# A convolution stage kept with features on partitions: centring folded into weights, variance by a matrix product

## Chip, cores and metric

One core of one Trainium2 chip runs the whole program. The metric is the device time of one execution in microseconds (us); less is better. The engines are TensorE (PE, its weight loads PEld), VectorE (DVE), ScalarE (ACT), GpSimd (POOL) and SyncE (SP, which issues the transfers).

## What is computed

The program is a chain of eight stages on 1024 tokens of 512 features, each followed by a residual sum and a layer norm. The change is in one of them, the convolution stack:

```python
h = einsum('blv,dv->bld', x, Win) + bin                 # 512 features to 64
def body(h, p):                                         # four layers
    y = silu(layernorm(h, l1w, l1b))
    y = sconv(y, phz, last_conv)                        # a recurrence along the tokens
    h = h + y * scl
    y = layernorm(h, l2w, l2b)
    y = silu(einsum('bld,fd->blf', y, w1) + b1_)        # 64 to 256
    y = einsum('blf,df->bld', y, w2) + b2_              # 256 to 64
    return (h + y, None)
h = layernorm(h, lnl_w, lnl_b)
return einsum('bld,vd->blv', h, Wout) + bout            # 64 to 512
```

The stage has nine layer norms over 64 features: two in each layer and one at its end. In what follows LN n is the n-th of them, from 0 to 8; LN 2i begins layer i and LN 2i+1 stands between its convolution and its small MLP.

## The kernel before

The stages run one after the other, each in a block of its own in which every engine has its list of instructions; a block ends when all engines are through. The activations are held twice: `x_tok` (tokens on partitions) for residual and norm, and `x_feat` (features on partitions) as operand of the products. The convolution stage is `conv_stack` (from L1048); `Tail` (from L63) is the end that all stages share: for each of eight tiles of 128 tokens DVE adds the product to `x_tok` (L92), takes statistics (L98, L99), ACT the root (L108), DVE the reciprocal (L101) and the scaling (L102), PE turns the tile (L134) and ACT copies it to `x_feat` (L115). The stage after it, `two_loras`, begins with small products (L880).

Everything in `conv_stack` is float32. The 1024 tokens are two halves of 512. Before the change the residual `h` has tokens on partitions: 128 partitions, eight tiles of 64 features. The order of work:

- **Loads.** SP issues nine transfers (L1099 to L1106): `w_in`; `w_out` and `w1_all`, which have 97 rows each (64 features, a gap, and a row of ones at 96 that carries the bias); `w2`; `cols`; `last_cols`; and three that are broadcast to all partitions. All but the first count on one semaphore, and DVE (L1285), ACT and POOL wait for the whole of it before their first instruction of the stage. Then SP issues the loads of the two stages to come (`load_ahead`).
- **Input.** PE makes `h` in 32 products of 64 columns (L1158).
- **A norm** (`norm`, L1272 to L1282): per half, DVE sums over features, divides, subtracts, squares, sums, scales; POOL raises the variance to the power -1/2 (L1134); DVE multiplies, into two copies where the convolution follows, since it wants real and imaginary part on 128 partitions.
- **Turning.** PE transposes four tiles of a half (L1170) and ACT applies weight and bias as it reads the bank: Silu into `y` (L1230), or Identity into `normed` (L1223).
- **Convolution.** DVE multiplies `y` by a table (L1300), runs a scan along the tokens (L1302) and multiplies by the table again (L1305); the scan of the second half starts from the last column of the first. PE folds the two parts back in products of 64 columns that also turn the result (L1180), and DVE adds it to `h` (L1309).
- **MLP.** PE multiplies by `w1` (L1189, 97 rows, two blocks of 128 outputs for each half), ACT applies Silu (L1237), PE multiplies by `w2` in 32 products of 64 columns (L1196) that turn the result again, DVE adds it and the bias (L1313, L1314).
- The four layers are a loop on each engine (`Fori`); POOL copies the layer's weights to a fixed place (L1141, L1144). After the last norm PE multiplies by `w_out` (L1209) and the tail begins.

## Time and profile before

| what | value |
|---|---|
| time, median of 3 runs | 1447.14 us (1446.95 to 1448.77) |
| the profiled execution | 1452.08 us, of which the trace spans 1450.3 us |
| PE busy | 1274.3 us, 88% of the span |
| DVE busy | 744.3 us, 51% |
| ACT busy | 431.1 us, 30% |
| POOL busy | 151.3 us, 10% |
| convolution stage, first transfer issued to last tile turned | 632.0 to 816.9 us |

A row of the trace gives the start in us from the start of the span, the duration, the engine, the line, the operation, output<-input, shape and count; in square brackets stands how long the engine was idle before and what released it. "PEclk" is the granted clock of TensorE as a share of 2.4 GHz: 1.00 is that level, 0.50 is 1.2 GHz. One float32 product leaves two rows of the trace on PE, so "x4" there are two products.

### The profile page before, as it was taken

Reading aid. Unit: us, or ns where it says so; the run is one execution under the profiler, and the core shown is the slowest. Engines: PE = TensorE matmul, PEld = TensorE weight load, DVE = VectorE, ACT = ScalarE, POOL = GpSimd, SP = SyncE. Lnnn points to the kernel's source line nnn. Section 1 sums busy time; section 2 is a strip of 40 time slices with the busy share of each in tenths; the row PEclk is TensorE's granted clock in tenths of the full one; section 3 lists DMA queues with packets and bytes.
Section 4 is the critical chain, followed back from the end, with each engine's and each line's share of the span. In section 5 each row is a group of like instructions: output and inputs, shape, how many; then the busy total and the mean of one; then the engine's idle time right before and its main releaser. Section 6 shows DMA issues by size and latency. Waiting matters only on the chain. (4 is left out here: it accounts for less than half of the span.)

```text
span 1450.3 us, 14475 instructions
## 1 busy us (share of the span) xinstructions
PE 1274.3 (88%) x5250; PEld 831.9 (57%) x5250; DVE 744.3 (51%) x1297; ACT 431.1 (30%) x717; POOL 151.3 (10%) x208
## 2 busy tenths in 40 slices
PE   7999998799799989973656788989999999799998
PEld 4787665344578778762434243444454443488876
DVE  5222323484776545414565564877776642433264
ACT  2122212120311224201222112146666666322141
POOL 0000000000394000001111013001101114000000
PEclk9999999899899999965665799989999999899999
DMA  7110000730355620003000000000000000111000
GB/s 311 44 43 0 0 0 18 308 145 1 131 196 195 219 85 1 0 31 128 0 0 0 0 22 23 0 1 2 1 2 3 2 3 1 44 66 70 17 22 37
DMA packets 18681, 78.82 MB, mean 54 GB/s; under 512 B 3330, under 2 KB 4226, under 8 KB 16452
## 3 DMA queue, kind: packets, MB, share of 16 engines
q1 hardware_dynamic: 18628, 78.13, 14.7%
q8 instruction: 32, 0.52, 0.1%
q14 instruction: 21, 0.17, 0.0%
HBM read 75.76 MB, written 2.10 MB: 54 GB/s over the span
## 5 line engine op out<-in xcount | busy, mean ns | idle before, releaser
L373 PE MATMUL psum<-L_ffn_x,L_ffn_w_up 128*128 128x512 f32 x1152 | 264.4, 391 | 3.2 <-DVE L_ffn_hidden L502 3.2
L373 PEld LDWEIGHTS psum<-L_ffn_x,L_ffn_w_up 128*128 128x128 f32 x1152 | 217.0, 189 | 50.2 <-DVE L_ffn_hidden L502 5.1
L1818 DVE TENSOR_REDUCE mqa_top<-psum 128x1 f32<-128x512 f32 (+3 forms) x304 | 186.0, 656 | 57.4 <-PE psum L1644 37.7
L1737 ACT ACTIVATE mqa_prob<-psum 128x512 f32<-128x512 f32 x288 | 159.8, 601 | 85.7 <-PE psum L1662 84.5
L390 PE MATMUL psum<-L_ffn_wd,L_ffn_part_h 128*128 128x512 f32 x600 | 142.6, 399 | 7.0 <-DVE L_ffn_wd L298 7.0
L1662 PE MATMUL psum<-mqa_stack,mqa_keys 100*128 100x512 f32 x288 | 132.7, 476 | 4.7 <-DMA mqa_stack<-mqa_rows 3.4
L390 PEld LDWEIGHTS psum<-L_ffn_wd,L_ffn_part_h 128*128 128x128 f32 x600 | 115.0, 193 | 31.9 <-DVE L_ffn_part_h L289 7.8
L1633 PE MATMUL psum<-mqa_keys,mqa_stack 96*128 96x512 f32 (+1 forms) x256 | 107.4, 439 | 2.3 <-DVE mqa_top L1818 1.0
L373 PE MATMUL psum<-L_attn_x,L_attn_w_up 128*128 128x512 f32 x456 | 105.4, 393 | 3.9 <-DVE L_attn_hidden L502 3.9
L373 PEld LDWEIGHTS psum<-L_attn_x,L_attn_w_up 128*128 128x128 f32 x456 | 86.7, 190 | 22.5 <-issue 4.3
L1662 PEld LDWEIGHTS psum<-mqa_stack,mqa_keys 100*128 100x128 f32 x288 | 55.3, 196 | 72.0 <-ACT mqa_prob L1737 62.6
L502 DVE TENSOR_TENSOR L_ffn_hidden<-L_ffn_gate,psum 128x512 f32 (+1 forms) x50 | 34.3, 686 | 100.0 <-PE psum L373 93.6
L108 ACT ACTIVATE ln_std<-ln_mean_var,eps 128x1 f32<-128x1 f32 x56 | 16.5, 295 | 218.0 <-DVE ln_mean_var L99 218.0
L1675 PE MATMUL psum<-mqa_prob,mqa_v 128*32 128x512 f32 x576 | 77.7, 605 | 0.0
L1170 PE MATMUL psum<-ident,conv_twice 128*128 128x128 f32 x72 | 20.1, 434 | 57.2 <-DVE conv_twice L1282 57.2
L1565 POOL TENSOR_SCALAR_AFFINE_SELECT mqa_prob<-mqa_prob 128x512 f32<-128x512 f32 x64 | 39.8, 640 | 266.9 <-ACT mqa_prob L1737 266.9
L415 ACT CAST L_ffn_w_up<-L_ffn_stage 128x1024 fp32r<-128x1024 f32 x25 | 26.3, 1050 | 134.0 <-DVE L_ffn_stage L479 95.8
L1633 PEld LDWEIGHTS psum<-mqa_keys,mqa_stack 96*128 96x128 f32 x256 | 50.7, 198 | 22.9 <-DVE mqa_top L1818 14.4
L289 DVE TENSOR_TENSOR L_ffn_part_h<-L_ffn_hidden,L_ffn_part_h 128x896 fp32r<-128x896 f32 (+2 forms) x32 | 31.7, 991 | 59.0 <-ACT L_ffn_part_h L286 59.0
L390 PE MATMUL psum<-L_attn_wd,L_attn_part_h 128*128 128x512 f32 x240 | 61.1, 407 | 0.0
L422 ACT ACTIVATE L_ffn_gate<-psum 128x512 f32<-128x512 f32 x50 | 29.8, 596 | 87.7 <-PE psum L373 64.6
L92 DVE TENSOR_TENSOR x_tok<-x_tok,psum 128x512 f32<-128x512 f32 x48 | 32.8, 683 | 40.2 <-PE psum L644 17.9
(245 smaller groups left out, 1663.4 us busy)
## 6 DMA issues: line engine op xcount, KB each, us to landing
L_ffn_stage<-in_L_w SPq DMA_DIRECT2D x25, 768.0 KB, 6.3
L_ffn_z_int<-in_L_z SPq DMA_DIRECT2D x14, 768.0 KB, 4.5
L_ffn_s_all<-in_L_s SPq DMA_DIRECT2D x14, 768.0 KB, 6.2
lora_wo<-in_L_wo SPq DMA_DIRECT2D x8, 1024.0 KB, 8.8
L_attn_stage<-in_L_w SPq DMA_DIRECT2D x10, 512.0 KB, 3.6
L_attn_w_down<-in_L_down SPq DMA_DIRECT2D x1, 2560.0 KB, 24.4
x_feat<-in_x_feat SPq DMA_DIRECT2D x2, 1024.0 KB, 7.3
x_tok<-in_x_tok SPq DMA_DIRECT2D x1, 2048.0 KB, 18.9
```

The costliest lines, as they stand in the source:

```text
L92: nc.vector.tensor_tensor(row, row, self.out_bank[t % 2][:, :], ALU.add).then_inc(self.out_taken, 1)
L289: nc.vector.tensor_tensor(part_h[:, g, 1, 0:n, :], src, part_h[:, g, 0, 0:n, :].bitcast(F32), ALU.subtract).then_inc(h_lo, 1)
L373: ins = nc.tensor.matmul(bank[half][:, :], w_up[:, slot, w_part, at:at + P], x[:, x_part, k, half * HALF:(half + 1) * HALF], start=k == 0 ...
L390: ins = nc.tensor.matmul(tail.out_bank[t % 2][:, :], part_h[:, g, h_part, f - groups[g].start, :], wd[:, w_part, f, :], start=f == 0 and n ...
L422: nc.scalar.activation(gate[:, :], g_bank[half][:, :], ACT.Silu).then_inc(gated, 1)
L502: nc.vector.tensor_tensor(hidden[:, f, half * HALF:(half + 1) * HALF], gate[:, :], u_bank[half][:, :], ALU.mult).then_inc(product, 1)
L1565: nc.gpsimd.affine_select(out=tile, in_=tile, compare_op=ALU.is_ge, fill=0.0, base=0, pattern=[[0, 4], [1, P]], channel_multiplier=-1).the ...
L1633: ins = nc.tensor.matmul(out[:, 0:width], stack[0:SPLIT, heads[0] // 2, cols(qt)], keys[0:SPLIT, heads[0] % 2, lo:lo + width], start=True, ...
L1662: ins = nc.tensor.matmul(score_bank[n % 3], keys[0:SHIFTED, head, cols(kt)], stack[0:SHIFTED, 4 * g:4 * g + 4, cols(qt)], start=True, stop ...
L1675: nc.tensor.matmul(value_bank[row:row + 32, :], v[:, kt, :], prob[:, n % PROBS, :], start=kt == 0, stop=final).then_inc(value_done, 1)
L1737: nc.scalar.activation(prob[:, n % PROBS, :], score_bank[n % 3], ACT.Exp, scale=SCALE)\
L1818: nc.vector.tensor_reduce(top[:, i % 2, lo // HALF, heads[0]:heads[-1] + 1], max_bank[n % 3][:, 0:len(heads) * width] .rearrange("p (h k) ...
```

## The change

The work of the stage is laid out anew; what it computes is the same.

- **Residual.** It lives with features on partitions, in two banks (`z_bank`, one for each half, 128 rows: the 64 features twice), as its centred part only. Centring is a product with a 128 x 128 matrix `centre` (POOL makes it, a memset and three selects), which is folded into the weights once at the start: `in_c` and `w2_c` by products, `back_c` (with the layer's scale) and `w1_s` by eight multiplications on POOL. The biases become per-feature columns: `adds` (sums of biases, four small DVE additions), `offset` and `b1_s` (nine small products and two DVE instructions).
- **Norm** (`deviation` and `normalise`), per half of 512 tokens: ACT squares the bank with `offset` added (64 rows), ACT copies the bank to `kept`, PE multiplies the squares by a constant matrix of 1/64, which gives the variance of each token on all 128 rows, ACT takes the root, DVE takes the reciprocal of 512 elements per partition, and one DVE instruction adds the offset and multiplies. POOL, the transposes, the sums and the second copy are gone.
- **Carry.** Before the next sum PE multiplies `kept` by the identity into the same bank, with which the accumulation begins; the convolution's product (one of 512 columns per half) and the MLP's two (`w2_c`) are added to it there. DVE no longer adds them.
- **Order.** On PE, in each layer: product of half 0, variance of half 0, the same for half 1, carry 0 and 1, `w1_s` of both halves, `w2_c` of both halves, then variance 0 and 1, carry 0 and 1. On ACT Square, copy, Sqrt of half 0 come ahead of those of half 1. On DVE the two halves of a norm come ahead of the convolution's multiplications and scans.
- **Loads** are four: the 64 x 512 of `Win`, a 128 x 35 array of all small parameters, 64 x 2048 of `W1` and `W2`, and `w_out` (97 rows), which only the last products wait for.
- The four layers are written out, without loops.

The diff, cut: what the lines printed above do is taken out throughout, and of what is added the core stands here.

```diff
@@ conv_stack: sync
+                sp.dma_start(low[:, 0:DIM], a["C_low"][:, 0:DIM]).then_inc(low_loaded, 16)
+                sp.dma_start(par[:, :], a["C_par"]).then_inc(loaded, 16)
+                sp.dma_start(low[:, DIM:], a["C_low"][:, DIM:]).then_inc(loaded, 16)
+                sp.dma_start(w_out[:, :], a["C_out"]).then_inc(out_loaded, 16)
...
@@ conv_stack: gpsimd
+                nc.gpsimd.memset(centre[:, :], -1.0 / LOW).then_inc(const, 1)
...
+                nc.gpsimd.memset(mean_of[:, :], 1.0 / LOW).then_inc(const, 1)
+                pool.wait_ge(loaded, 32)
+                for i in range(C_DEPTH):
+                    nc.gpsimd.tensor_scalar(back_c[:, i, :], centre[:, :], cols[:, i, 4:5], None, ALU.mult)\
+                        .then_inc(scaled, 1)
+                    nc.gpsimd.tensor_scalar(w1_s[:, i, :], w1[:, i, :], cols[0:LOW, i, 2:3], None, ALU.mult)\
+                        .then_inc(scaled, 1)
...
@@ conv_stack: tensor
+                pe.wait_ge(low_loaded, 16)
+                pe.wait_ge(const, 4)
+                for k in range(KC):
+                    ins = nc.tensor.matmul(var_bank[0][:, k * P:(k + 1) * P], w_in[:, k * P:(k + 1) * P],
+                                           centre[0:LOW, :], start=True, stop=True)
+                ins.then_inc(in_made, 1)
...
+                def variance(n, half):
+                    pe.wait_ge(square_ready[half], n + 1)
+                    nc.tensor.matmul(var_bank[half], mean_of[:, :], square[:, halves[half]], start=True, stop=True)\
+                        .then_inc(var_ready[half], 1)
+                def carry(n, half):
+                    pe.wait_ge(kept_ready[half], n + 1)
+                    nc.tensor.matmul(z_bank[half], c.ident[:, :], kept[:, halves[half]], start=True, stop=False)
+                pe.wait_ge(in_ready, 1)
+                start(0, range(KC))
+                start(1, range(0, 2))
+                pe.wait_ge(const, 5)
+                pe.wait_ge(small_ready, 2)
+                variance(0, 0)
+                start(1, range(2, KC))
+                variance(0, 1)
+                for half in range(2):
+                    carry(0, half)
+                for i in range(C_DEPTH):
+                    pe.wait_ge(scaled, 2 * i + 2)
+                    for half in range(2):
+                        pe.wait_ge(back_ready[half], i + 1)
+                        nc.tensor.matmul(z_bank[half], back_c[:, i, :], back[:, halves[half]],
+                                         start=False, stop=True).then_inc(z_ready[half], 1)
+                        variance(2 * i + 1, half)
+                    for half in range(2):
+                        carry(2 * i + 1, half)
+                    for half in range(2):
+                        pe.wait_ge(norm_ready[half], 2 * i + 2)
+                        if i == 0 and half == 0:
+                            pe.wait_ge(w2_ready, 2)
+                        for f in range(FT):
+                            nc.tensor.matmul(ff_bank[2 * half + f], w1_s[:, i, f * P:(f + 1) * P],
+                                             norm[0:LOW, halves[half]], start=True, stop=True).then_inc(ff_ready, 1)
+                    for half in range(2):
+                        for f in range(FT):
+                            pe.wait_ge(hidden_ready, 4 * i + 2 * half + f + 1)
+                            ins = nc.tensor.matmul(z_bank[half], w2_c[:, i, f, :], hidden[:, f, halves[half]],
+                                                   start=False, stop=f == FT - 1)
+                        ins.then_inc(z_ready[half], 1)
+                    for half in range(2):
+                        variance(2 * i + 2, half)
+                    for half in range(2):
+                        if i < C_DEPTH - 1:
+                            carry(2 * i + 2, half)
+                pe.wait_ge(out_loaded, 16)
...
+                    pe.wait_ge(last_ready, t // (NT // 2) + 1)
...
@@ conv_stack: scalar
+                def deviation(n):
                     for half in range(2):
+                        act.wait_ge(z_ready[half], n + 1)
+                        nc.scalar.activation(square[:, halves[half]], z_bank[half][0:LOW, :], ACT.Square,
+                                             bias=offset[0:LOW, n // 2:n // 2 + 1]).then_inc(square_ready[half], 1)
+                        nc.scalar.copy(kept[:, halves[half]], z_bank[half]).then_inc(kept_ready[half], 1)
+                        act.wait_ge(var_ready[half], n + 1)
+                        nc.scalar.activation(std[:, halves[half]], var_bank[half], ACT.Sqrt,
+                                             bias=c.eps[:, 0:1]).then_inc(std_ready[half], 1)
+                for i in range(C_DEPTH):
+                    deviation(2 * i)
                     for half in range(2):
+                        act.wait_ge(norm_ready[half], 2 * i + 1)
+                        nc.scalar.activation(y[:, halves[half]], norm[:, halves[half]], ACT.Silu,
+                                             scale=cols[:, i, 0:1], bias=cols[:, i, 1:2]).then_inc(y_ready[half], 1)
+                    deviation(2 * i + 1)
                     for half in range(2):
                         for f in range(FT):
                             act.wait_ge(ff_ready, 4 * i + 2 * half + f + 1)
+                            nc.scalar.activation(hidden[:, f, halves[half]], ff_bank[2 * half + f], ACT.Silu,
+                                                 bias=b1_s[:, i * FT + f:i * FT + f + 1]).then_inc(hidden_ready, 1)
+                deviation(LAST)
+                for half in range(2):
+                    act.wait_ge(norm_ready[half], LAST + 1)
+                    nc.scalar.activation(normed2[0:LOW, halves[half]], norm[0:LOW, halves[half]], ACT.Identity,
+                                         scale=last_cols[:, 0:1], bias=last_cols[:, 1:2]).then_inc(last_ready, 1)
                 tail.act(act)
...
@@ conv_stack: vector
+                def normalise(n, rows):
                     for half in range(2):
+                        dve.wait_ge(std_ready[half], n + 1)
+                        then(nc.vector.reciprocal(inverse[rows, halves[half]], std[rows, halves[half]]))
+                        dve.wait_ge(kept_ready[half], n + 1)
+                        nc.vector.scalar_tensor_tensor(norm[rows, halves[half]], kept[rows, halves[half]],
+                                                       offset[rows, n // 2:n // 2 + 1], inverse[rows, halves[half]],
+                                                       ALU.add, ALU.mult).then_inc(norm_ready[half], 1)
+                for i in range(C_DEPTH):
+                    normalise(2 * i, slice(0, P))
+                    for half in range(2):
+                        part = halves[half]
+                        dve.wait_ge(y_ready[half], i + 1)
                         then(tt(turned[:, part], y[:, part], rot.wave[:, i, part], ALU.mult))
...
+                        tt(back[:, part], state[:, part], rot.wave[:, i, part], ALU.mult)\
+                            .then_inc(back_ready[half], 1)
+                    normalise(2 * i + 1, slice(0, LOW))
+                normalise(LAST, slice(0, LOW))
...
```

## Rows read from the trace of the kernel before

**Rows 1.** Busy time by stage: start of the stage, one layer, last layer to first tail sum

```profile
core 0: us, PE busy (x) PEld busy (x) DVE busy (x) ACT busy (x) POOL busy (x), PEclk, DMA share, GB/s
631.50:662.40 30.90, 13.92 (x64) 13.73 (x64) 0.04 (x1) 0.05 (x1) 2.63 (x6) 0.50 0.40 116
668.40:698.30 29.90, 17.49 (x73) 12.48 (x73) 17.87 (x42) 6.77 (x9) 4.92 (x7) 0.61 0.01 4
```

**Rows 2.** Timeline, start of the stage: transfers issued, input products, first sum

```profile
631.97 0.34 SPq L1099 DMA_DIRECT2D conv_w_in<-in_C_in  x1
...
633.48 6.50 SPq L1102 DMA_DIRECT2D conv_w<-in_C_w  x1
634.28 13.73 PEld L1158 LDWEIGHTS psum<-conv_w_in,x_feat 128*128 128x128 f32 x64 [3.76 <-DMA conv_w_in<-in_C_in]
...
662.36 0.88 DVE L1290 TENSOR_TENSOR conv_h<-psum,conv_rows 128x256 f32<-128x256 f32 x2 [32.48 <-DMA conv_rows<-in_C_bin]
```

**Rows 3.** Transfers of the start: size and median us to landing

```profile
two_low<-in_L_low SPq DMA_DIRECT2D x1, 256.0 KB, 5.0
two_high<-in_L_high SPq DMA_DIRECT2D x1, 256.0 KB, 10.8
...
conv_w_in<-in_C_in SPq DMA_DIRECT2D x1, 128.0 KB, 2.3
```

**Rows 4.** The page's part 6: a transfer of 512 KB in the first stage

```profile
L_attn_stage<-in_L_w SPq DMA_DIRECT2D x10, 512.0 KB, 3.6
```

**Rows 5.** Timeline of the first layer: from the norm's last row to the convolution's product

```profile
669.54 0.78 ACT L1230 ACTIVATE conv_y<-psum,conv_col 128x512 f32<-128x512 f32 x1 [4.06 <-PE psum L1170]
...
670.45 0.69 DVE L1300 TENSOR_TENSOR conv_turned<-conv_y,wave 128x512 f32<-128x512 f32 x1 [0.79 <-ACT conv_y L1230]
...
672.61 0.69 DVE L1305 TENSOR_TENSOR conv_back<-conv_state,wave 128x512 f32<-128x512 f32 x1
...
673.45 1.97 PE L1180 MATMUL psum<-conv_fold_sc,conv_back 128*128 x8 [2.61 <-DVE conv_back L1305]
```

**Rows 6.** Reciprocals and their like on DVE: ns least/median/most

```profile
L1842 DVE RECIPROCAL mqa_inv<-psum x16: 245/249/258, 992.8 to 1241.5; 128x16 f32<-128x16 f32 x16
...
L968 DVE RECIPROCAL rot_small<-rot_small x1: 178/178/178, 319.0 to 319.0; 128x4 f32<-128x4 f32 x1
...
L978 DVE RECIPROCAL rot_small<-rot_small x1: 170/170/170, 320.9 to 320.9; 128x4 f32<-128x4 f32 x1
...
L1797 DVE SCALAR_TENSOR_TENSOR mqa_q_lo<-psum,mqa_bq,mqa_q_hi 128x512 fp32r<-128x512 f32 x8 | 6.0, 746 | 8.7 <-ACT mqa_q_hi L1725 8.7
```

**Rows 7.** ACT: two switches of table around a Tanh; a Silu; a copy

```profile
320.62 1.28 ACT L945 ACT_TABLE_LOAD   x1
321.92 0.21 ACT L945 ACTIVATE decay<-rot_small 128x4 f32<-128x4 f32 x1
322.14 1.28 ACT L108 ACT_TABLE_LOAD   x1
...
719.86 0.60 ACT L1237 ACTIVATE conv_hidden<-psum 128x512 f32<-128x512 f32 x1 [0.27 <-PE psum L1189]
720.90 1.28 ACT L1230 ACT_TABLE_LOAD   x1 [0.44 <-POOL conv_col L1144]
...
L115 ACT COPY x_feat<-psum 128x512 f32<-128x512 f32 x48 | 27.4, 571 | 11.7 <-PE psum L134 11.7
```

**Rows 8.** Timeline of the stage's end: products of 512 columns and the tail's sums

```profile
791.32 3.78 PE L1209 MATMUL psum<-conv_w_out,conv_normed 97*128 97x512 f32 x4 [0.86 <-ACT conv_normed L1223]
...
793.43 0.69 DVE L92 TENSOR_TENSOR x_tok<-x_tok,psum 128x512 f32<-128x512 f32 x1 [4.15 <-PE psum L1209]
...
802.39 1.02 PE L1209 MATMUL psum<-conv_w_out,conv_normed 97*128 97x512 f32 x2
...
812.35 0.68 DVE L92 TENSOR_TENSOR x_tok<-x_tok,psum 128x512 f32<-128x512 f32 x1
```

**Rows 9.** PE alone in the first layer's MLP and after it

```profile
core 0: us, PE busy (x), PEclk, DMA share, GB/s
...
684.60:688.00 3.40, 3.40 (x6) 0.50 0.00 0
688.00:691.50 3.50, 3.50 (x24) 0.98 0.02 5
...
694.90:698.30 3.40, 0.01 (x1) 0.51 0.00 0
```

**Rows 10.** Timeline of the last layer: the convolution's product of half 0

```profile
764.16 1.97 PE L1180 MATMUL psum<-conv_fold_sc,conv_back 128*128 x8 [2.62 <-DVE conv_back L1305]
```

More of the change, by code:

```diff
@@ L1285, in _ @@
-                dve.wait_ge(loaded, LOADS)
+                    dve.wait_ge(step, count)
+                tt = nc.vector.tensor_tensor
+                dve.wait_ge(loaded, 32)
+                for i in range(C_DEPTH):
+                    ins = tt(adds[:, i + 1:i + 2], adds[:, i + 1:i + 2], adds[:, i:i + 1], ALU.add)
+                    if i < C_DEPTH - 1:
+                        then(ins)
+                ins.then_inc(adds_ready, 1)
+                dve.wait_ge(small_made, 1)
+                nc.vector.tensor_copy(offset[:, :], var_bank[1][:, 0:C_DEPTH + 1]).then_inc(small_ready, 1)
@@ L1300, in _ @@
+                for i in range(C_DEPTH):
+                    normalise(2 * i, slice(0, P))
+                    for half in range(2):
+                        part = halves[half]
+                        dve.wait_ge(y_ready[half], i + 1)
                         then(tt(turned[:, part], y[:, part], rot.wave[:, i, part], ALU.mult))
[L1301 to L1303 removed]
+                        before = rot.start[:, i:i + 1] if half == 0 else state[:, HALF - 1:HALF]
+                        then(nc.vector.tensor_tensor_scan(state[:, part], rot.decay[:, i:i + 1].to_broadcast([P, HALF]),
```

263 lines of the change are left out of this document (80 added, 183 removed).

## Prediction

> **What bounds the kernel now.** I read the page first: PE is busy for most of the span, but that mean says nothing of this stage. So I read the busy times by stage. In the first 31 us of the stage DVE and ACT do nothing; in a layer of 29.9 us PE is busy 17.5 us at a granted clock of 0.61, DVE 17.9 us, ACT 6.8 us [rows 1]. No engine is full: the stage is one chain of waits from engine to engine. What a change is worth here is read from the length of that chain, in three pieces.
>
> - The head. PE has its operands at 634.3 and its input products done 13.7 us later, but DVE's first sum comes only at 662.36, released by the last of the broadcast loads; SP needed 6.5 us to issue `w2` alone [rows 2]. The first convolution product of half 0 (the "mark" in what follows) ends at 673.45 + 1.97 = 675.42 [rows 5].
> - The layers. The same product of the last layer starts at 764.16 [rows 10], so a layer takes (764.16 - 673.45) / 3 = 30.24 us.
> - The end. From its end, 766.13, to the tail's first sum at 793.43 [rows 8] are 27.30 us. After that each tile's sum follows the one before, up to 812.35, and nothing of that changes.
>
> **Prices.** All from rows of one profiled execution of 1452.08 us, which stands 4.9 above the median of 1447.14; I forecast the change of the chain and take it from the median.
>
> *Reciprocal of 512 elements per partition, new, 18 of them.* The nearest rows take 170 and 178 ns for 4 elements and 249 ns for 16 [rows 6]. That is (249 - 174) / 12 = 6.25 ns an element, and 174 + 508 x 6.25 = 3.35 us for 512. The two bounds: 0.69 us, if it went like the 512-element multiplication [rows 5] and the 16-element one were slow for its own reasons; and above, 258 ns against 170 gives 7.3 ns an element, 3.9 us. I take 3.35, since both nearest rows are reciprocals. A rule speaks for more: the Trainium skill, "VectorE: DVE Perf Modes", "First, the fixed hardware budget", says that the reciprocal is an iterated division with a repeat count of 8. Eight cycles at the page's 0.96 GHz are 8.33 ns an element, 4.4 us by the same sum. By it 16 elements would take 174 + 12 x 8.33 = 274 ns; the row's longest took 258, so the trace speaks against it.
>
> *The second DVE instruction* has three operands and takes 0.75 [rows 6]. One norm on DVE is then 2 x (3.35 + 0.05 + 0.75) = 8.3 us, against some 6 before: DVE's part of a norm gets longer, not shorter.
>
> *ACT.* Silu without pointer operands takes 0.60 [rows 7] and with two of them 0.78 [rows 5]; Square and Sqrt have one, 0.69. The copy takes 0.57 and a table load 1.28 [rows 7]. Sqrt and Silu want different tables (a load stands between them before as well), so every layer has four loads, written out where before it had one. Those ahead of a Silu lie beside DVE's 8.3 us. Those ahead of the first Sqrt of a norm stand behind the copy, with the variance product running beside them: nothing else hides them. The lead of a norm, bank ready to reciprocal started, is 0.05 + 0.69 + 0.57 + 1.28 + 0.69 + 0.05 = 3.33 us. A switch is taken at 1.28 because one is followed at once by its Tanh and that by the next load [rows 7]. The Trainium skill, "ScalarE: Activation LUTs", "What ACT_TABLE_LOAD costs", has about 2.66 us a switch, with a drain of 1.38 behind the load; by it each lead would be 4.7 us. The row shows no such gap.
>
> *PE.* A float32 product of 512 columns that waits for its operand takes 793.43 - 791.32 = 2.1 us at the half clock, 0.05 of it the hop to its reader, so 2.05; at full clock 1.02 [rows 8]. Two in a run at half clock take 3.78, so a second one adds 1.7 [rows 8], and half of that, 0.85, at full clock. A layer has 18 of them: 15.3 us of work at 2.4 GHz, 30.7 at 1.2. So the clock decides more than before. The rows show when it moved: PE ran the MLP's products without a pause at 0.50 up to 688, had 0.98 after that, and was back at 0.51 in a stretch in which it idled [rows 9]. In the new layer PE idles some 7 us while DVE does LN 2i and the scans, so I take the convolution's product at the half clock; then it is nearly always at work (products, variances, carries), and I take one of the four MLP products on the chain at the half clock and the others at full: 2.05 + 3 x 0.85 = 4.6 us.
>
> *Convolution on DVE.* Unchanged: multiplication, scan, multiplication of half 0 take 672.61 + 0.69 - 670.45 = 2.85 [rows 5]. It now waits for both halves of the norm, which its place in the 8.3 us includes.
>
> **The sum.** A new layer, mark to mark: LN 2i+1, 3.33 + 8.3 = 11.6; MLP 4.6 (its end for half 0 is on the chain, that of half 1 is awaited by nobody for 3 us); LN 2i+2, 11.6; convolution 2.85 + 0.1 + 2.05 = 5.0. That is 32.8 us against 30.24: **2.56 worse in each of three layers, +7.7.** DVE is at work 4 x 4.1 + 2 x 2.65 = 21.7 of them, so it comes nearest to a bound.
>
> The head: `Win` is first in the queue and lands as before, 634.3 (2.3 us [rows 3]); four products of 128 columns, 0.5 each (0.43 for 64 columns: 13.73 us for 32 [rows 2]), end at 636.3. The third transfer is issued at about 633.1 and has 512 KB, 3.6 us in [rows 4], so 636.7; four small additions on DVE, 0.8; nine products of one to five columns, 0.4 each, and eight of 128 columns, 0.5 each, all in PE's order ahead of the input product: it starts at 645.1. Four products, two at half and two at full clock, 5.1: 650.2. Behind two more and the variance, 2.55; Sqrt and hops 0.8; DVE 8.3; convolution 5.0: the mark is at 666.8 against 675.4, **-8.6**.
>
> The end: 11.6 + 4.6 + 11.6 + 0.05 = 27.85 against 27.30, **+0.55**.
>
> Costed at nothing: POOL's eight multiplications start at 637 and are wanted at 664; nothing waits for POOL then. The carries (two products each time) lie beside DVE's 8.3 us; without that cover, 1.7 to 3.4 each time. `w_out`, 97 rows, is wanted 155 us after its issue. The loads of later stages are issued some 15 us sooner, behind all that this stage wants. Input copy and `w2_c` copies on ACT lie beside PE's work.
>
> Sum: -8.6 + 7.7 + 0.55 = -0.4, and 1447.14 - 0.4 = **1446.7 us**: head start and dearer norms cancel.
>
> **Rivals.** A difference under 0.2% (2.9 us) can't be told from none here.
>
> - *The clock stays up* (0.22). If 18 long products keep it at 2.4 GHz, convolution and MLP cost 1.0 less each: layer 30.8, mark at 665.8, end 26.85: -9.6 + 1.7 - 0.45 = -8.4, 1438.8. For it: the products are four times as long as those of 64 columns before. Against: PE's pause of 7 us, and what an idle stretch did to the clock [rows 9].
> - *The clock stays down through the MLP* (0.10), the slower side. At 1.2 GHz the four products take 7.15, and variance 0, which stands in PE's order behind the `w2_c` products of half 1, comes 5.1 us after the bank instead of inside the lead: 2.55 + 2.56 for each of four layers, +20.4, 1467. It decides from the point where more than two of the eight MLP products of a layer are at the half clock. For it: 0.61 is the mean clock of a layer now [rows 1].
> - *Reciprocal by eight cycles* (0.05): 4.42 instead of 3.35, 18 of them on the chain, +19.3, 1466. The page's rule from above.
> - *Reciprocal cheap* (0.06): at 0.69 us a norm is bound by ACT, 6.9 to the second Sqrt's end and 1.5 behind: 8.4 instead of 11.6, nine times, 1418.
> - *A drain at each table switch* (0.04): 1.38 more in eight leads, +11.0, 1457.7. The skill's other rule, against the row.
> - *The head start isn't had in full* (0.07): a 64-row load took 10.8 us where others were ahead of it [rows 3]. Then the small products start 7 us later, 1453.9.
> - *The forecast* (0.46). Its own range is 1441 to 1452: 15 hops a layer, each 0.05 or more, and one product more or less at half clock.
>
> **How the numbers follow.** Range 1436 to 1468: it leaves out the cheap reciprocal alone, with the edges of the others. Faster by over 0.2%: 0.22 + 0.06 + 0.14 of the forecast's case = 0.42. Slower: 0.10 + 0.05 + 0.04 + 0.07 + 0.10 = 0.36. Within: 0.22.
>
> **What would show it.** DVE's reciprocal row at 3.35 for 512 elements; a layer of 32.8 with DVE busy 21 to 22; table loads behind each copy with Sqrt at once behind them; input product started at 645; clock under 0.6 at the convolution's product and full in the MLP. I am wrong if the reciprocal is under 3 us, if a layer is under 31 or over 35, or if the mark isn't within 2 us of 666.8.

## The result and the profile after

The kernel after the change takes 1456.33 us (median of 5 runs, 1454.3 to 1458.01), the kernel before 1447.23 (5 runs, 1446.95 to 1448.77): ratio 1.0059, 95% interval 1.0044 to 1.0074. It is slower by some 9 us; I had forecast 1446.7, no change, as the likeliest.

The profiled executions took 1456.33 and 1452.08 us. I cut the stage as in the prediction: head (first transfer issued to mark, which is the end of the first convolution product of half 0), layer (a third of the time from that product's start to its start in the last layer), end (from its end in the last layer to the tail's first sum). Behind that stand 23.9 us in both, the rest of the tail up to the next stage's first row on DVE.

| us | head | layer | end | stage |
|---|---|---|---|---|
| before | 43.45 | 30.24 | 27.30 | 185.37 |
| forecast | 34.8 | 32.8 | 27.85 | 185.0 |
| after | 36.72 | 33.91 | 29.15 | 191.48 |

So the stage is 6.1 us longer: -6.7 + 3 x 3.67 + 1.85. All three pieces came out above the forecast. The rest of the profiled execution is 1.9 us shorter after the change, so the 9.1 us between the medians are not all found in this pair of traces.

The busy times of the three layers (after), beside 17.5 for PE, 17.9 for DVE and 6.8 for ACT in a layer of 29.9 us in [rows 1]:

```profile
core 0: us, PE busy (x) PEld busy (x) DVE busy (x) ACT busy (x) POOL busy (x), PEclk, DMA share, GB/s
667.00:701.00 34.00, 25.16 (x36) 7.99 (x36) 21.69 (x15) 17.00 (x23) 0.00 (x0) 0.70 0.00 0
701.00:735.00 34.00, 25.35 (x36) 7.99 (x36) 21.51 (x15) 16.80 (x23) 0.00 (x0) 0.70 0.00 0
735.00:769.00 34.00, 25.48 (x36) 8.03 (x36) 21.41 (x15) 16.72 (x23) 0.00 (x0) 0.70 0.00 0
```

Every engine but POOL has more to do than before. What DVE does is 21.4 to 21.7 us a layer, as worked out; but PE, with 25.2 to 25.5, is the busiest. DVE's costliest group in the stage:

```profile
line engine op names shapes xcount | busy us, mean ns | idle before us <-releasers
L1296 DVE RECIPROCAL conv_inverse<-conv_std 64x512 f32<-64x512 f32 (+1 forms) x18 | 60.2, 3346 | 61.0 <-ACT conv_std L1244 61.0
...
L1298 DVE SCALAR_TENSOR_TENSOR conv_norm<-conv_kept,conv_offset,conv_inverse 64x512 f32<-64x512 f32 (+1 forms) x18 | 13.4, 747 | 0.6
```

The timeline (after) of LN 1, from the product that ends at the mark to the MLP, and the start of LN 2:

```profile
664.86 2.05 PE L1191 MATMUL psum<-conv_back,conv_back_c 128*128 128x512 f32 x2 [6.11 <-DVE conv_back L1311]
...
666.67 0.69 DVE L1311 TENSOR_TENSOR conv_back<-conv_state,wave 128x512 f32<-128x512 f32 x1
666.95 0.68 ACT L1240 ACTIVATE conv_square<-psum,conv_offset 64x512 f32<-64x512 f32 x1 [4.03 <-PE psum L1191]
...
667.68 2.07 PE L1169 MATMUL psum<-conv_square,conv_mean_of 64*128 64x512 f32 x2 [0.77 <-ACT conv_square L1240]
668.12 1.28 ACT L1244 ACT_TABLE_LOAD   x1
...
669.69 2.07 PE L1191 MATMUL psum<-conv_back,conv_back_c 128*128 128x512 f32 x2
669.79 0.69 ACT L1244 ACTIVATE conv_std<-psum,eps 128x512 f32<-128x512 f32 x1 [0.39 <-PE psum L1169]
670.51 3.35 DVE L1296 RECIPROCAL conv_inverse<-conv_std 64x512 f32<-64x512 f32 x1 [3.15 <-ACT conv_std L1244]
...
674.53 3.78 PE L1175 MATMUL psum<-conv_kept,ident 128*128 128x512 f32 x4
674.64 0.69 ACT L1244 ACTIVATE conv_std<-psum,eps 128x512 f32<-128x512 f32 x1 [1.69 <-PE psum L1169]
...
675.36 3.35 DVE L1296 RECIPROCAL conv_inverse<-conv_std 64x512 f32<-64x512 f32 x1 [0.72 <-ACT conv_std L1244]
...
678.24 3.96 PE L1201 MATMUL psum<-conv_norm,conv_w_s 64*128 64x512 f32 x8
...
678.74 0.74 DVE L1298 SCALAR_TENSOR_TENSOR conv_norm<-conv_kept,conv_offset,conv_inverse 64x512 f32<-64x512 f32 x1
...
684.15 0.68 ACT L1240 ACTIVATE conv_square<-psum,conv_offset 64x512 f32<-64x512 f32 x1 [1.23 <-PE psum L1206]
...
687.64 3.35 DVE L1296 RECIPROCAL conv_inverse<-conv_std 128x512 f32<-128x512 f32 x1 [8.15 <-ACT conv_std L1244]
```

Four things are to be seen. The table load ends at 669.40 and Sqrt starts at 669.79, released by PE: it was the variance product that set the lead, not the load. `back` of half 1 was ready at 667.36, but its product starts at 669.69, since variance 0 stands ahead of it in PE's order; so the second Sqrt comes late and DVE idles 0.72. Then PE, not DVE, is what the MLP waits for: half 0 of the norm is ready at 674.63, but PE has the second variance and the carries in hand till 678.3; and half 1 is ready at 679.48, before PE comes to its products, the second half of the row at 678.24, at some 680.3. (In LN 2, from 684.1 on, it is the other way round: DVE works without a pause from 687.64 to the scans.) And all of LN 1 runs at the half clock:

```profile
core 0: us, PE busy (x) PEld busy (x) DVE busy (x) ACT busy (x) POOL busy (x), PEclk, DMA share, GB/s
648.00:664.00 16.00, 9.98 (x22) 3.42 (x20) 10.00 (x6) 6.59 (x9) 0.00 (x0) 0.93 0.13 52
664.00:676.00 12.00, 9.59 (x10) 2.83 (x11) 7.99 (x7) 5.62 (x8) 0.00 (x0) 0.50 0.00 0
676.00:684.00 8.00, 8.00 (x16) 2.87 (x15) 3.45 (x2) 3.38 (x5) 0.00 (x0) 0.83 0.00 0
684.00:690.00 6.00, 4.65 (x10) 1.61 (x9) 2.36 (x1) 4.59 (x7) 0.00 (x0) 0.92 0.00 0
690.00:698.00 8.00, 2.92 (x4) 0.67 (x2) 7.86 (x7) 3.17 (x4) 0.00 (x0) 0.71 0.00 0
```

The head (after), against [rows 2]:

```profile
630.19 0.57 SPq L1107 DMA_DIRECT2D conv_low<-in_C_low  x1
...
631.44 0.48 SPq L1109 DMA_DIRECT2D conv_low<-in_C_low  x1
...
636.60 0.83 DVE L1280 TENSOR_TENSOR conv_par<-conv_par 64x1 f32<-64x1 f32 x4 [8.16 <-DMA conv_low<-in_C_low]
...
637.99 3.55 PE L1148 MATMUL psum<-conv_par,conv_low 64*128 64x1 f32 x16
...
641.40 3.76 PE L1155 MATMUL psum<-conv_centre,conv_low 64*128 64x128 f32 x16
...
645.09 1.22 PE L1162 MATMUL psum<-x_feat,conv_in_c 128*128 128x512 f32 x1
```

### The profile page after: what moved, and what is told of

Read it like the earlier page. It is cut to its first block and busy times, and to the rows that moved or that the text cites. A ratio compares the mean times of both kernels' runs of the same rounds, so it can differ in the third digit from the quotient of the medians.

```text
span 1454.6 us, 13818 instructions
## 1 busy us (share of the span) xinstructions
PE 1307.4 (90%) x5094; PEld 811.0 (56%) x5096; DVE 760.7 (52%) x1177; ACT 475.1 (33%) x777; POOL 134.9 (9%) x187
## 5 line engine op out<-in xcount | busy, mean ns | idle before, releaser
L1296 DVE RECIPROCAL conv_inverse<-conv_std 64x512 f32<-64x512 f32 (+1 forms) x18 | 60.2, 3346 | 61.0 <-ACT conv_std L1244 61.0
L502 DVE TENSOR_TENSOR L_ffn_hidden<-L_ffn_gate,psum 128x512 f32 (+1 forms) x50 | 34.3, 685 | 99.3 <-PE psum L373 93.1
L502 DVE TENSOR_TENSOR L_attn_hidden<-L_attn_gate,psum 128x512 f32 (+1 forms) x20 | 13.8, 688 | 75.9 <-PE psum L373 75.2
## 6 DMA issues: line engine op xcount, KB each, us to landing
x_tok<-in_x_tok SPq DMA_DIRECT2D x1, 2048.0 KB, 18.4
```

What stands on the lines that cost most here:

```text
L502: nc.vector.tensor_tensor(hidden[:, f, half * HALF:(half + 1) * HALF], gate[:, :], u_bank[half][:, :], ALU.mult).then_inc(product, 1)
L1296: then(nc.vector.reciprocal(inverse[rows, halves[half]], std[rows, halves[half]]))
```

## The experiments

The theory after the result: the new layout's price is the reciprocal of 512 elements; its gain, in the head, comes from the loads and not from the layout; the table loads are hidden; the clock decides a few us. Head, layer and end are taken as above. The stage is measured by itself: the three pieces don't add up to it exactly, since the marked product takes 1.1 to 2.05 us by the clock, and the rest of the tail 23.9 to 24.8. Rivals: table loads (the prediction had 1.28 of each lead on the chain), the clock, the number of products and hops. Stages are from the profiled executions, medians and intervals from all runs against the kernel before on the same chip.

| kernel | head | layer | end | stage | median us | ratio to before (95%) |
|---|---|---|---|---|---|---|
| e0_before_again | 43.38 | 29.92 | 28.21 | 185.26 | 1450.28 | 1.0007 (0.9988 to 1.0026) |
| e1_no_recip | 34.12 | 30.53 | 26.37 | 176.35 | 1441.50 | 0.9942 (0.9918 to 0.9965) |
| e2_no_table | 36.80 | 33.85 | 29.14 | 192.31 | 1456.94 | 1.0063 (1.0039 to 1.0086) |
| e3_warm5 | 35.81 | 33.69 | 28.45 | 189.58 | 1452.01 | 1.0028 (1.0004 to 1.0051) |
| e4_lnexp | 37.97 | 36.83 | 36.78 | 209.49 | 1478.76 | 1.0222 (1.0182 to 1.0263) |
| e5_before_loads | 29.49 | 28.80 | 27.97 | 167.78 | 1440.04 | 0.9943 (0.9918 to 0.9968) |
| e6_lnexp_keep | 36.96 | 34.33 | 29.89 | 193.73 | 1464.01 | 1.0120 (1.0082 to 1.0158) |
| e7_w2_later | 33.35 | 33.92 | 29.18 | 188.49 | 1454.05 | 1.0034 (1.0015 to 1.0053) |
| e9_small | 34.12 | 28.66 | 28.98 | 173.04 | 1434.66 | 0.9901 (0.9876 to 0.9927) |
| e10_small_later | 36.80 | 28.94 | 28.97 | 176.19 | 1445.43 | 0.9980 (0.9952 to 1.0007) |
| e11_out_last | 32.60 | 29.66 | 28.87 | 174.70 | 1440.44 | 0.9936 (0.9919 to 0.9953) |
| e12_small_between | 30.49 | 30.60 | 26.88 | 174.19 | 1439.55 | 0.9929 (0.9905 to 0.9953) |

**e0_before_again** is the kernel before, unchanged.

> The kernel before, unchanged, for a second profile and for the scatter. The profile shown stands 4.9 us above its median. If the stage's length varies by itself (TensorE's clock rises and falls at other points of the layer), this profile shows a stage shorter than 185.4 us by 3 to 5 us where the execution is near the median, with the same operations; if the surplus lay elsewhere, the stage is 185.4 again.

Its profiled execution took 1451.6 us with a stage of 185.26, against 185.37 in the other one: these two stages agree to 0.1 us, their pieces to 0.9 (end 27.30 and 28.21). Both executions are from the upper part of the scatter (the kernel before took 1443 to 1454 us in all these comparisons), so no trace shows the stage of an execution near the median, and the question that this run was to answer stays open. What lies outside the stage, the same code in every kernel here, took 1260.2 to 1267.8 us from trace to trace.

**e1_no_recip.** It leaves the reciprocal out: a constant is written in its place.

```diff
-then(nc.vector.reciprocal(inverse[rows, halves[half]], std[rows, halves[half]]))
+then(nc.vector.tensor_scalar(inverse[rows, halves[half]], std[rows, halves[half]], 0.0, 1.0, ALU.mult, ALU.add))
```

> Leaves out the 18 reciprocals of the changed kernel: DVE writes a constant 1 in their place with an instruction of some 0.5 us (the norm is then not divided by the deviation). Theory A, the reciprocal is what made a norm dearer: it is on the chain in the norms ahead of a convolution (LN 0, 2, 4, 6, 8), about 4 us each, and nearly covered by PE's carries in the odd ones, so the kernel is 18 to 24 us faster than the changed one, about 1435. Theory B, TensorE's clock is what made it dearer and the reciprocals lie beside PE's work: under 8 us.

The stage is 15.1 us shorter than after the change, less than the 18 to 24 of theory A and far more than B's 8; the granted clock of a layer is no higher, 0.67 against 0.70. DVE's instruction takes 0.42 in place of 3.35, 5.9 a norm, 53 us over nine norms, so most of the relief is stopped by something else. Timeline (e1_no_recip) of LN 1:

```profile
663.72 2.05 PE L1191 MATMUL psum<-conv_back,conv_back_c 128*128 128x512 f32 x2 [3.85 <-DVE conv_back L1311]
...
669.37 0.42 DVE L1296 TENSOR_SCALAR conv_inverse<-conv_std 64x512 f32<-64x512 f32 x1 [3.15 <-ACT conv_std L1244]
...
673.39 3.46 PE L1175 MATMUL psum<-conv_kept,ident 128*128 128x512 f32 x4
...
674.67 0.74 DVE L1298 SCALAR_TENSOR_TENSOR conv_norm<-conv_kept,conv_offset,conv_inverse 64x512 f32<-64x512 f32 x1
676.78 3.70 PE L1201 MATMUL psum<-conv_norm,conv_w_s 64*128 64x512 f32 x8
```

LN 1 is ready at 675.41, but PE has the carries in hand till 676.8. From the mark (665.77) to the MLP's first product are 11.0 us, with the reciprocal 11.3: in the odd norms it costs next to nothing, since PE's own queue is the bound there. The gain is in the even ones: from LN 2's first Square to the next layer's convolution product are 11.8 us (682.43 to 694.25) in place of 14.5. And with no reciprocal at all a layer still takes 30.53, not less than before.

**e2_no_table.** It leaves the root out, so that ACT keeps one table within the layers.

```diff
-nc.scalar.activation(std[:, halves[half]], var_bank[half], ACT.Sqrt,
+nc.scalar.activation(std[:, halves[half]], var_bank[half], ACT.Identity,
```

> Leaves out the root: ACT applies Identity (same operands) in place of Sqrt, so that no table is loaded between the Silus. Prediction's sum had the load ahead of Sqrt on the chain in eight norms, 1.28 each: 10 us faster than the changed kernel. The trace of the changed kernel shows Sqrt waiting for the variance product after the load has ended (0.3 to 0.4 us): by that reading the loads are covered and the gain is under 1.5 us.

No table is loaded behind the first Silu's, up to the tail, and head, layers and end together are 0.1 us shorter. (The stage is 0.8 us longer, since a load of 1.28 now stands ahead of the tail's first root.) The 1.28 us that the prediction put on the chain in each lead was hidden by the variance product.

**e3_warm5.** Five products that nobody reads, in PE's pause before the convolution's products:

```diff
+for _ in range(5):
+    nc.tensor.matmul(ff_bank[0], c.ident[:, :], rot.wave[:, 0, 0:HALF], start=True, stop=True)
 for half in range(2):
     pe.wait_ge(back_ready[half], i + 1)
```

> Adds five products of 512 columns on PE, into a bank that is free then, ahead of the wait for the convolution's operand in each layer, so that PE does not idle there. Nothing else differs. Theory B (the clock is the loss): granted clock near 1.0 at the convolution's product, 1.0 us less there, and 0.7 to 1 us less in the norm behind it, 6 to 10 us in all: 1447 to 1450. Theory A (the reciprocal is the loss): the convolution's product alone gets cheaper, 3 to 5 us in all. If the clock does not follow, no gain, or up to 1 us a layer slower where the five products run at the half clock and end after the operand is there.

Busy times (e3_warm5), the stretches of the last fence above:

```profile
664.00:676.00 12.00, 8.32 (x16) 2.53 (x16) 10.11 (x8) 7.07 (x10) 0.00 (x0) 1.00 0.00 0
676.00:684.00 8.00, 6.23 (x7) 2.33 (x8) 1.68 (x2) 1.81 (x3) 0.00 (x0) 0.51 0.00 0
```

The odd norm is now at 2.4 GHz: its second reciprocal starts at 673.60 without a pause, and MLP work begins at 673.73 instead of 678.24. But now PE waits for DVE in this norm too:

```profile
677.77 3.77 PE L1203 MATMUL psum<-conv_norm,conv_w_s 64*128 64x512 f32 x4 [2.06 <-DVE conv_norm L1300]
```

Then the clock is at half just where the MLP runs, and this first layer is no shorter (35.1). The third, with 0.95 of the clock from start to end, takes 32.5 against 34.0 after the change. So a high clock is worth some 1.5 us a layer here, and the stage gains 1.9 in all; the clock doesn't bring the layer back to 30.

**e7_w2_later.** In the changed kernel, the eight products that centre `W2`, and ACT's two copies, move from before the input product to behind the first norm's variances.

> The changed kernel with the eight products that centre the second MLP weight (3.76 us on PE at the half clock) behind the input's products and variances instead of ahead of them, and ACT's two copies of them behind the first norm's roots. Theory: they lie on the head's chain, and the mark comes 3 to 4 us sooner; nothing else moves. Rival: the clock rises only later then, since those products helped to bring it up, and the mark comes less than 1.5 us sooner.

The head is 3.4 us shorter (36.72 to 33.35), layer and end stay: these products were on the chain of the head.

**e4_lnexp and e6_lnexp_keep.** The power -1/2 on ACT, as exp(-0.5 ln v), with no reciprocal; in the second DVE also takes over the copy to `kept`.

```diff
-nc.scalar.activation(std[:, halves[half]], var_bank[half], ACT.Sqrt,
-                     bias=c.eps[:, 0:1]).then_inc(std_ready[half], 1)
+nc.scalar.activation(std[:, halves[half]], var_bank[half], ACT.Ln,
+                     bias=c.eps[:, 0:1]).then_inc(ln_ready, 1)
+act.wait_ge(ln_ready, 2 * n + half + 1)
+nc.scalar.activation(inverse[:, halves[half]], std[:, halves[half]], ACT.Exp,
+                     scale=-0.5).then_inc(std_ready[half], 1)
```

> The changed kernel with the reciprocal square root made by ACT alone, exp(-0.5 ln(v + eps)), in place of Sqrt on ACT and the reciprocal on DVE. Theory A (the reciprocal's 3.35 us is the price of the new norm): nearly all that leaving it out gave comes back, less 0.65 us of Exp for each half: stage of 179 to 183 us against 191.5, median 1443 to 1448. If Ln and Exp stand in different tables, two more loads in each norm, 1.28 each, take the gain away.

> As the one before, and DVE, now idle in the norm, makes the copy of the bank that ACT made. ACT's chain is shorter by 0.57 in each half where the variance product does not end later anyway, the even norms: stage 3 to 6 us shorter than with the copy on ACT, 174 to 179 us, median 1438 to 1443.

ACT's groups in the stage (e4_lnexp):

```profile
L1245 ACT ACT_TABLE_LOAD x18 | 23.1, 1283 | 0.3
L1248 ACT ACT_TABLE_LOAD x18 | 23.1, 1283 | 0.3
```

A table is loaded before every Ln and every Exp, 36 loads, 46 us; with the copy taken off ACT the stage is still 2.3 us above that of the change. (The mean layer of e4 holds a third one of 40.9 us, at a granted clock of 0.62; the other two take 35.3 and 34.3.) Both are misses, and say nothing on a version without these loads.

**e5_before_loads and e11_out_last** take the kernel before and touch its loads only: `w_out` last, on a semaphore of its own that the last products wait for; e5 also splits `w1_all` into 96 rows and one.

```diff
-for dst, src in ((w_out, "C_out"), (w1_all, "C_w1"), (w2, "C_w2"), (cols, "C_cols"),
-                 (last_cols, "C_last")):
+sp.dma_start(w1_all[0:ONE, :, :], a["C_w1"][0:ONE]).then_inc(loaded, 16)
+sp.dma_start(w1_all[ONE:ONE + 1, :, :], a["C_w1"][ONE:ONE + 1]).then_inc(loaded, 16)
+for dst, src in ((w2, "C_w2"), (cols, "C_cols"), (last_cols, "C_last")):
...
+sp.dma_start(w_out[:, :], a["C_out"]).then_inc(out_loaded, 16)
```

> The kernel before with one part of the change: its loads in an order and shape like those of the change (the small MLP's weights as 96 rows and one row instead of 97 rows, the output weights last and on a semaphore of their own). Theory: the head start of the change comes from the loads alone, and the old layout can have it too: DVE's first sum comes when PE has the input ready, some 13 to 14 us sooner, 1433 to 1435. Rival: the broadcast rows and small arrays were the slow ones, or loads of later stages take the place: under 5 us gained.

> The kernel before, with only one of the two edits of e5_before_loads: w_out (97 rows) is loaded last, on a semaphore of its own, and w1_all stays one transfer of 97 rows. Theory A, each transfer of 97 rows moves at some 27 GB/s behind which the broadcast loads queue, so one of the two accounts for its bytes: w_out has 194 KB of 582, about a third of the 14 us of the head: head 38 to 40 us against 43.45, median 1441 to 1444. Theory B, what counted was that w_out is not waited for: the head is 30 us as in e5_before_loads. Theory C, it is w1_all alone that blocks the queue: the head stays at 43.

The transfer view over 630 to 664 us (40 slices of 0.85 us), first of the kernel before, then of e5_before_loads:

```profile
GB/s 0 0 0 111 70 22 19 24 27 27 24 27 111 229 27 24 29 24 24 38 34 50 157 149 30 29 51 126 289 251 188 231 328 330 258 166 274 397 424 395
```

```profile
GB/s 0 0 0 0 0 0 212 217 296 215 65 165 122 24 156 308 193 186 306 354 330 311 318 355 383 318 311 308 349 424 318 19 27 27 24 29 29 19 29 29
```

Before, the queue moves 25 to 29 GB/s in two stretches of 6 us each between 634 and 648, with the broadcasts behind. The mean busy share of the 16 DMA engines is 0.07 and 0.08 there, not much above what one engine alone would give (1/16). SP needs 6.50 us to issue `w2` [rows 2]. In e5 it needs 0.36, and DVE's first sum, at 650.71, is released by PE and not by a load:

```profile
635.41 0.36 SPq L1104 DMA_DIRECT2D conv_w<-in_C_w  x1
```

The head falls by 14.0 us in e5 and by 10.9 in e11, so most of it is `w_out`, 97 rows, ahead in the queue and in the wait; the two can't be told apart, since e11 moves it out of both. The head of e11, 32.6, fits none of its theories, but is nearest to B. The rest of e5's stage, 1.4 us less in each layer for the same code, goes with the clock, 0.68 in two of its three layers where before has 0.61 (e5_before_loads, first layer):

```profile
661.70:690.10 28.40, 16.00 (x72) 11.98 (x72) 17.86 (x43) 6.78 (x9) 4.91 (x6) 0.68 0.01 3
```

The medians of the two don't differ. Both beat the kernel before and the changed one. By them the loads give 7 to 9 us, less than the 10.7 (e11) and 17.6 (e5) that the stage loses in the traces; where the rest of e5's goes isn't shown.

**e9_small.** The changed kernel, the reciprocal taken where it is small:

```diff
-nc.tensor.matmul(var_bank[half], mean_of[:, :], square[:, halves[half]], start=True, stop=True)\
-    .then_inc(var_ready[half], 1)
+for t in range(HT):
+    at = (half * HT + t) * P
+    ins = nc.tensor.matmul(var_bank[half][:, t:t + 1], square[:, at:at + P], mean_of[:, 0:1],
+                           start=True, stop=True)
+ins.then_inc(var_ready[half], 1)
...
-then(nc.vector.reciprocal(inverse[rows, halves[half]], std[rows, halves[half]]))
+then(nc.vector.reciprocal(inv[:, at], root[:, at]))
+tt(diag[:, at, :], c.ident[:, :].unsqueeze(1).to_broadcast([P, HT, P]),
+   inv[:, at].unsqueeze(2).to_broadcast([P, HT, P]), ALU.mult).then_inc(diag_ready[half], 1)
...
+nc.tensor.matmul(var_bank[half], ones[:, :],
+                 diag[:, half * HT:(half + 1) * HT, :].rearrange("p t n -> p (t n)"),
+                 start=True, stop=True).then_inc(spread_ready[half], 1)
```

Four products of one column per half give the variance with tokens on partitions, the reciprocal is of 128 x 4, and DVE's product with the identity puts these four numbers on a diagonal of 128 x 512, which the product with ones spreads over all rows. In the odd norms this last product of half 0 stands ahead of variance 1 in PE's order, that of half 1 between the carries.

> The changed kernel with the reciprocal taken where it is small. The variance comes out with tokens on partitions (four products of one column per half, the tile of squares as the fixed operand), Sqrt and reciprocal are of 4 elements per partition, DVE writes the four numbers on a diagonal (512 elements), and one more product with a matrix of ones spreads them over all rows of the variance's bank. The result is the same. Theory A, the dearer norm is the 512-element reciprocal: DVE has 0.17 + 0.7 in place of 3.35 per half, so a norm gets shorter although a product, a DVE instruction and two hops are added, as far as the carries at half clock let it (writing a constant in place of the reciprocal gave 15.1 of the stage): stage 172 to 180 us against 191.5, median 1438 to 1446. Theory B, what counts is the number of products and hops between engines in a norm, and the reciprocal is only where the wait shows: the added product (1.0 to 2.05) and hops take back what DVE gives, stage 187 or more, median 1450 or more.

Timeline (e9_small) of LN 1, half 0:

```profile
665.85 1.05 PE L1177 MATMUL psum<-conv_mean_of,conv_square 64*128 64x1 f32 x8 [0.77 <-ACT conv_square L1262]
666.28 1.28 ACT L1266 ACT_TABLE_LOAD   x1
...
667.58 0.26 ACT L1266 ACTIVATE conv_root<-psum,eps 128x4 f32<-128x4 f32 x1
667.87 0.18 DVE L1319 RECIPROCAL conv_inv<-conv_root 128x4 f32<-128x4 f32 x1 [1.39 <-ACT conv_root L1266]
668.09 0.69 DVE L1320 TENSOR_TENSOR conv_diag<-ident,conv_inv 128x512 f32<-128x512 f32 x1
...
668.83 1.99 PE L1183 MATMUL psum<-conv_diag,conv_ones 128*128 128x512 f32 x2 [0.24 <-DVE conv_diag L1320]
...
670.86 0.74 DVE L1326 SCALAR_TENSOR_TENSOR conv_norm<-conv_kept,conv_offset,psum 64x512 f32<-64x512 f32 x1 [2.08 <-PE psum L1183]
```

The stage is 18.4 us shorter than after the change, in the range of theory A, though the norm has one product, one DVE instruction and two hops more; 1434.66 us is below that theory's range and the fastest median of all. Not all of the 18.4 is the reciprocal's: the granted clock of the three layers is 0.93, 0.79 and 0.94, where after the change it is 0.70. The layer falls to 28.66, where the kernel before and its variants with other loads have 28.80 to 30.24: the new layout is no longer dearer, and not clearly cheaper either. Against e5 the two measures disagree, stage 173.04 against 167.78, ratio 0.9901 against 0.9943 with intervals that overlap, so which is faster stays open. Here Sqrt follows the table load, which ends at 667.56, at once.

**e10_small_later and e12_small_between** are e9_small with the `W2` products moved, as in e7_w2_later, or in two groups into pauses of PE with ACT's copies behind the first Silus.

> As e9_small, with the products that centre the second MLP matrix, and ACT's two copies of them, moved behind the first norm's products. By theory A, with the head a term of its own: 2 to 4 us less than e9_small, all of it ahead of the first convolution product, the rest of the stage as there. If those products only filled a wait for the loads, the same as e9_small within 1 us.

> e9_small, with the products that centre the second MLP matrix put into two pauses of PE (before the second spreading product of the first norm, and behind the first carries), and ACT's copies of them behind the Silus of the first layer. In e10_small_later these copies stood ahead of the first Silu, which waited for them till 663.1. Theory A, only that wait cost it its gain: head 31 to 32.5 us against 34.12 of e9_small and 36.80, the rest as e9_small, stage 170 to 172, median 1431 to 1434. Theory B, the products are on the chain wherever they stand before the first convolution product, since PE has no pause of 1.9 us there: head 34 to 36, median 1434 to 1437.

e10 is a miss: with the short norm the first Silu is ready sooner, and ACT's copies stood ahead of it, waiting for PE. The head is 2.7 us longer than in e9. Its median is 10.8 us above that of e9, though, with times from 1435 to 1452; the trace, of an execution of 1439.39, doesn't show where the rest lies. e12 has the head of theory A or a little less, 30.49, but not its stage: the gain is given back in the third layer. The starts of the marked product lie 27.66, 30.98 and 27.35 us apart in e9, and 27.58, 30.95 and 33.27 in e12. Busy times, first of e9_small, then of e12_small_between:

```profile
720.00:750.00 30.00, 22.72 (x69) 10.67 (x69) 14.10 (x22) 15.72 (x23) 0.00 (x0) 0.94 0.00 1
```

```profile
720.00:750.00 30.00, 27.85 (x67) 13.61 (x68) 8.60 (x15) 14.24 (x21) 0.00 (x0) 0.72 0.00 1
```

The same layer, at clock 0.94 in one and 0.72 in the other. That the shift of the head moved the clock's phase is argued, not shown. These layers also say what the short reciprocal is worth at either level: at 0.94 its layer takes 27.4 where e3's, with the long one, took 32.5 at 0.95; at 0.74 (the whole of e12's third layer) it takes 33.3 where the changed kernel's takes 33.9 at 0.70. It is PE's queue that is long in the second case.

## Why the prediction was wrong

**What changed, in two terms.** The kernel before with better loads alone has a stage of 174.7 (e11) or 167.8 (e5), the one before 185.4, the changed one 191.5. The changed kernel's loads hold that repair too (`w_out` last, no broadcasts), so by these traces the loads give 11 to 18 us and the layout costs 17 to 24: 4 to 7 in the head, 13 to 15 in the layers, the rest at the end (by the medians some 8 and 17). The reciprocal is the largest part of what the layout costs: e1 takes 15.1 of it back with the clock no higher, e9 18.4 with the clock's help. The prediction had a gain in the head and dearer layers, with the right signs, but their sum at -0.4 where the traces have +6.1.

**Right.** The reciprocal: 3.35, from a line through 4 and 16 elements, between the bounds of 0.69 and 3.9; that it fits to the hundredth is luck. The repeat count of 8 that the Trainium skill, "VectorE: DVE Perf Modes", "First, the fixed hardware budget", gives for the reciprocal, read as eight cycles an element (4.4 us by the prediction's estimate), does not hold here. The second instruction: 0.75. LN 2 on DVE takes 8.2 (8.3), convolution 4.8 (5.0). The clock at half in the convolution and up in the MLP. From the input product to the mark 21.8 us, as forecast (645.1 to 666.8). No drain stands behind a table load (e9's timeline), against the Trainium skill, "ScalarE: Activation LUTs", "What ACT_TABLE_LOAD costs", with its 1.38.

**The head, 1.9 us short (34.8 forecast, 36.72).** The step that failed is the loads' landing: DVE's small additions start 6.4 us after the first issue (630.19 to 636.60), not 4.7. The price was one transfer's 3.6 us, taken as if the other two were not in front; from the third's issue at 631.44 it was 5.2. That the two in front made the difference is argued, not shown. In the span's own time the forecast looks right, 645.1 and 666.8 against 645.09 and 666.91, but only since this trace's stage began 1.8 us earlier: a forecast must be compared from the same origin. In costing nine small products and eight of 128 columns ahead of the input product it was right, and they were worth moving (e7).

**The layer, 1.1 us short (32.8, 33.9), all of it between the mark and the MLP's end.** This is the larger part of the miss, and the step that failed is the path through the odd norm. The sum let it run over DVE (3.33 and 8.3, then the MLP) and put the carries at nothing, since they "lie beside DVE's 8.3 us". They do lie beside it, but PE's queue is the longer one: second product, variance 1 and the carries (3.78) stand at the half clock, one behind the other, ahead of the MLP. So the MLP's first product starts 11.3 us after the mark, 3.6 after half 0 of its norm is ready, and half 1's norm is ready before PE wants it. From the mark to the MLP's sum of half 0 (684.1) are 17.2 us, not 11.6 + 4.6 = 16.2. That DVE's end of LN 1 lies 12.6 after the mark and the MLP's sum 4.6 behind that looks like a dearer norm and a right MLP, but is not the chain: e1, with 5.9 us less on DVE, starts the MLP only 0.3 sooner. I had put the convolution's product at half clock, and not followed that to the next products in PE's order. For the same reason DVE, with its 21.7 us, is not "nearest to a bound"; PE is, with 25.2.

Two mistakes nearly cancelled in the lead: the table load was named as exposed ("nothing else hides them") and is hidden (e2), while the variance product at half clock, 2.07, takes its place: 3.6 in place of 3.33. LN 2 took 11.7, its forecast 11.6.

**The end, 1.3 us short (27.85, 29.15).** The same stretch once more: from the last mark (768.65) to the MLP's sum of half 0 are 17.5 us, not 16.2. (The end varies by 0.9 between the two traces of the kernel before.)

**The baseline.** 1.9 + 3 x 1.1 + 1.3 = 6.5 us are the stage's part of the miss: -0.4 was forecast and +6.1 came. Of the 9.1 between the medians (interval 6.4 to 10.7) the other 3 are not found in the stage. I took the change of the chain from a median that the profiled execution exceeded by 4.9. Where that surplus lies isn't shown: e0's trace is of a long execution too, and outside the stage traces of the same code differ by 7.6. What sets that time stays open.

**The rivals.** None happened. "The clock stays up" is what e3 forced in part: 1.9 us in the stage where the rival had 8 below the forecast, and in the one layer that had 0.95 of the clock 1.5, where the rival had 2.0. "The clock stays down through the MLP" did not come: the clock was 0.83 over 676 to 684 us and 0.92 over 684 to 690. The head start not had in full is partly true, 1.9 of its 7. My chance for slower, 0.36, was too low: three terms were each built with every overlap granted, so their errors had one sign. The range, 1436 to 1468, holds the result, but its upper part stood there for rivals that didn't come; the forecast's own, 1441 to 1452, doesn't hold it. That the mark came at 666.91 where 666.8 was forecast is luck too: from the same origin it is 1.9 off.

## What to carry to other kernels

Before a layout is turned, ask how many elements per partition each slow operation then has: the reciprocal costs 6.5 ns for each, and with 128 tokens across partitions four did the work of 512. When a change also mends something apart from its idea (here the loads), try that alone on the old kernel: here it is more than half of what the best version has over the kernel before. And work that is put at nothing because it lies beside another engine's still stands in its own engine's queue: write down the start of every item of that queue, of both halves, at the clock that the row before it has.

## What was unexpected of the hardware

- A 97-row load at the head of the queue and in the wait cost 11 of the 14 us of e5. SP's issue of `w2` takes 6.50 us behind two loads of 97 rows (before), 2.69 behind one (e11) and 0.36 behind none (e5).
- RECIPROCAL takes 3.35 us for 512 elements with 64 partitions as with 128.
- Ln and Exp, one after the other, each had a table load of 1.28 us, 36 in a stage.
- A product of one column with a new fixed operand takes 0.26 us (e9, at 2.4 GHz), so that the variances of 512 tokens in four columns take 1.05, hardly less than the 1.12 of one product of 512 columns at that clock; but at 1.2 GHz the latter takes 2.07.
- Products added to keep the clock up lift it where they are and it falls later (e3, first layer: 1.00, then 0.51 in the MLP).
- The short reciprocal makes a layer some 5 us shorter where the granted clock is 0.94 (e9 against e3) and under 1 where it is 0.74 (e12 against the changed kernel).
